# Attention and gate kernel: V and the second query of slot 1 exchange banks and places

## What is computed

```
xn = layernorm(x)
q, k, v = xn @ wq.T, xn @ wk.T, xn @ wv.T          # 32, 8 and 8 heads of 128
q = q * cos + rotate_half(q) * sin ; k likewise
p = softmax(q @ k.T / sqrt(128) * scale + causal)   # four query heads share a k and v
s = (p @ v) @ wo.T
g = silu(sum over the top 2 of 4 experts: gate_e * (xn @ A_e.T @ B_e.T) * 4)
out = x + s * g
```

## Time and profile before

| | us |
|---|---|
| median of 3 runs | 1343.22 |
| lowest and highest run | 1341.77, 1343.50 |
| the profiled execution | 1342.1 |
| its span, first to last instruction | 1340.3 |
| PE, ACT, DVE, POOL busy in it | 1317.3, 971.7, 957.8, 419.9 |
| mean granted clock of PE | 0.994 |

### The profile page before, as it was taken

One profiled execution on the slowest core, in us unless ns is written; L12 is line 12 of the kernel. 1 busy time (PEld: TensorE's weight loads), 2 busy tenths in 40 slices (PEclk: granted clock), 3 DMA queues, 4 the chain that ended last, 5 costly groups with the idle time before them and its releaser, 6 DMA issues.

```text
span 1340.3 us, 22644 instructions
## 1 busy us (share of the span) xinstructions
PE 1317.3 (98%) x7000; PEld 1106.4 (83%) x7000; DVE 957.8 (71%) x2440; ACT 971.7 (72%) x2529; POOL 419.9 (31%) x341
## 2 busy tenths in 40 slices
PE   8899999999999999999999999999999999999996
PEld 7788788878888888888888888888888888888885
DVE  6777587766767677777767677776777767767775
ACT  6977577776768777777777776877777777777673
POOL 5323322333114332223414133141422334133321
PEclk9899999999999999999999999999999999999998
DMA  6000000111001000000101000010100000002223
GB/s 220 9 25 20 25 9 20 53 42 47 31 17 32 16 23 8 16 16 16 31 0 31 0 17 30 0 31 0 31 16 3 29 16 23 8 32 86 84 79 113
DMA packets 23530, 43.66 MB, mean 33 GB/s; under 512 B 2496, under 2 KB 2752, under 8 KB 23488
## 3 DMA queue, kind: packets, MB, share of 16 engines
q1 hardware_dynamic: 20896, 38.74, 9.0%
q10 hardware_dynamic: 2592, 4.40, 0.9%
HBM read 34.74 MB, written 8.39 MB: 32 GB/s over the span
## 4 chain that ended last, share of the span: by engine, by line
PE 94%; ACT 2%; DVE 2%; issue 1%; DMA 0%; ACTq 0%
PE bank_a L487 19%; PE bank_b L487 19%; PE bank_b L581 13%; PE o_ps L581 13%; PE pv_ps L574 10%; PE pair L558 8%; PE pair L565 6%; PE pair L554 2%; PE pair L556 1%; PE o_ps L487 1%; PE bank_a L544 1%; ACT x_sb L945 1%; PE o_ps L534 1%; DVE pT_lo L1204 0%; PE pair L487 0%
## 5 line engine op out<-in xcount | busy, mean ns | idle before, releaser
L391 POOL TENSOR_TENSOR rot<-rot,tab 128x512 f32<-128x512 f32 x160 | 206.7, 1295 | 601.2 <-ACT rot L803 600.9
L871 ACT ACTIVATE pT_hi<-pair 128x768 fp32r<-128x768 f32 x128 | 103.9, 812 | 168.5 <-PE pair L565 167.7
L852 ACT ACTIVATE probs<-probs,row_min 128x128 f32<-128x128 f32 (+1 forms) x512 | 225.6, 447 | 0.1
L863 ACT ACTIVATE probs<-probs,row_inv 128x128 f32<-128x128 f32 (+1 forms) x512 | 190.7, 446 | 22.7 <-DVE row_inv L1234 22.3
L1204 DVE TENSOR_TENSOR pT_lo<-pair,pT_hi 128x768 fp32r<-128x768 f32 x128 | 121.6, 950 | 92.3 <-ACT pT_hi L871 92.0
L374 POOL TENSOR_TENSOR w_hi<-raw,zero 128x512 fp32r<-128x512 f32 x74 | 84.2, 1138 | 247.0 <-PE bank_a L487 131.0
L487 PE MATMUL bank_a<-xT_hi,w_hi 128*128 (+1 forms) x376 | 153.0, 407 | 0.7 <-DVE xT_lo L1073 0.6
L487 PE MATMUL bank_b<-xT_hi,w_hi 128*128 (+1 forms) x376 | 150.3, 400 | 0.0
L1184 DVE TENSOR_TENSOR q_lo<-cosx,q_hi 128x512 fp32r<-128x512 f32 x128 | 117.0, 915 | 44.3 <-ACT q_hi L810 44.1
L487 PE MATMUL bank_a<-xT_hi,w_lo 128*128 (+1 forms) x376 | 146.9, 391 | 0.0
L487 PE MATMUL bank_b<-xT_hi,w_lo 128*128 (+1 forms) x376 | 146.8, 391 | 0.0
(11 more groups left out here) (177 smaller groups left out, 3246.1 us busy)
## 6 DMA issues: line engine op xcount, KB each, us to landing
raw<-w_seq SPq DMA_DIRECT2D x76, 256.0 KB, 2.6
gate_scratch<-b_raw ACTq DMA_DIRECT2D x16, 256.0 KB, 2.0
out<-y_sum SPq DMA_DIRECT2D x16, 256.0 KB, 2.1
x_sb<-x SPq DMA_DIRECT2D x3, 1024.0 KB, 10.8
mid<-x SPq DMA_DIRECT2D x8, 256.0 KB, 2.7
mid<-gate_scratch SPq DMA_DIRECT2D x8, 256.0 KB, 2.9
raw<-x SPq DMA_DIRECT2D x7, 256.0 KB, 2.6
raw<-gate_scratch SPq DMA_DIRECT2D x7, 256.0 KB, 2.8
```

The costliest lines, as they stand in the source:

```text
L391: nc.gpsimd.tensor_tensor(v, v, tab[:, s:s + SEQ].unsqueeze(1).to_broadcast([P, 2, SEQ]), ALU.mult).then_inc(sin_done[kind], 1)
L852: a = nc.scalar.activation(s, s, ACT.Exp, bias=row_min[:, j % 2, i:i + 1], scale=-1.0, accum_out=row_sum[:, i:i + 1])
L863: a = nc.scalar.activation(s, s, ACT.Copy, scale=row_inv[:, i:i + 1])
L871: nc.scalar.activation(pT_hi[:, :, :], pair[j % 2][:, :, 0:ROWS], ACT.Copy).then_inc(pThi_done, 1)
```

## The change

TensorE projects V first, into bank_b, and H2 second, into bank_a. So the projection H3 (bank_b) waits for V's copy instead of H2's cosine product, the projection K (bank_a), and in unit 30 the transposition of V, wait for H2's cosine product instead of V's copy. ScalarE's and VectorE's lists in every unit from 1 on are written in another order; in unit 0 only the copy of V comes ahead of H2's half copies. GpSimd's and SyncE's lists stay.

```diff
@@ -646,18 +646,18 @@
                     bank_free(H0, c2)
                 else:
                     pe.wait_ge(y_added, n4[0])
-                project(H2, bank_b, WQ + 2, x_1, w_1)
+                project(V, bank_b, WV, x_1, w_1)
             pe_side(u, 1, 2)
             if not last:
                 bank_free(H1, c2)
-                project(V, bank_a, WV, x_1, w_1)
+                project(H2, bank_a, WQ + 2, x_1, w_1)
             pe_side(u, 1, 3)
 
 
             pe.wait_ge(probs_ready, n4[3])
             turn_probs(2)
             if not last:
-                bank_free(H2, c2)
+                pe.wait_ge(vT_done, c2)
                 project(H3, bank_b, WQ + 3, x_1, w_1)
             pe_side(u, 2, 0)
             if not last:
@@ -669,7 +669,7 @@
             if ahead:
                 if isinstance(u, int) and u < BLOCKS - 2:
                     pe.wait_ge(xlo_done, BLOCK_TILES * (u + 3))
-                pe.wait_ge(vT_done, c2)
+                bank_free(H2, c2)
                 project(K, bank_a, WK, x_2, w_2)
             pe_side(u, 2, 2)
             if ahead:
@@ -888,51 +888,51 @@
             low_scores(2, n4[3])
             if not last:
                 q_high(H0, c2, n4[3])
-            rows_high(1, n4[2], n4[1])
             attn_high(0, n4[1], None if first else n4[-2])
             exponents(2, n4[3])
+            rows_high(1, n4[2], n4[1])
             act_side(u, 1, 0)
+            low_scores(3, n4[4])
             if not last:
                 swap_halves(H1, bank_a, c2, H0, c2)
-            low_scores(3, n4[4])
             act_side(u, 1, 1)
-            if not last:
-                k_high(c2, n4[4])
             normalise_rows(2, n4[3])
             attn_high(1, n4[2], None if first else n4[-2])
             if not last:
-                swap_halves(H2, bank_b, c2, K, c2)
+                k_high(c2, n4[4])
             act_side(u, 1, 2)
             if not last:
+                copy_vT(c2, c1, bank_b)
                 q_high(H1, c2, n4[3])
             act_side(u, 1, 3)
+            if not last:
+                swap_halves(H2, bank_a, c2, K, c2)
             rows_high(2, n4[3], n4[2])
             exponents(3, n4[4])
             act_side(u, 2, 0)
             if not last:
                 swap_halves(H3, bank_b, c2, H1, c2)
-                copy_vT(c2, c1)
                 low_scores(0, n4[5])
             act_side(u, 2, 1)
-            normalise_rows(3, n4[4])
             if not last:
                 q_high(H2, c2, n4[4])
             attn_high(2, n4[3], None if first else n4[0])
+            normalise_rows(3, n4[4])
             act_side(u, 2, 2)
-            if ahead:
-                swap_halves(K, bank_a, c3, H2, c2)
-            if is_unit(u, 1):
-                b_high()
             if not last:
                 q_high(H3, c2, n4[4])
             if ahead:
                 swap_halves(H0, bank_b, c3, H3, c2)
-            act_side(u, 2, 3)
             rows_high(3, n4[4], n4[3])
+            if ahead:
+                swap_halves(K, bank_a, c3, H2, c2)
             if not last:
                 exponents(0, n4[5])
                 low_scores(1, n4[6])
                 normalise_rows(0, n4[5])
+            act_side(u, 2, 3)
+            if is_unit(u, 1):
+                b_high()
             attn_high(3, n4[4], None if first else n4[0])
             if not last:
                 v_high(c2, n4[4])
@@ -1006,8 +1006,8 @@
             q_high(H1, 2, 3)
             normalise_rows(2, 3)
             act_side(0, 1, 2)
-            swap_halves(H2, bank_b, 2, K, 2)
-            copy_vT(2, 1)
+            copy_vT(2, 1, bank_b)
+            swap_halves(H2, bank_a, 2, K, 2)
             attn_high(1, 2, None)
             act_side(0, 1, 3)
             rows_high(2, 3, 2)
@@ -1265,69 +1265,69 @@
                          start=isinstance(u, int) and u - b < BLOCKS, final=final, bank=(o_ps, bank_b)[t][:, :], xg_set=t)
 
             rows_low(0, n4[1])
+            mask_rows(2, n4[3])
+            attn_low(0, n4[1])
+            if not last:
+                q_low(H0, c2)
             if not first:
                 tile_in(1, 0)
-            mask_rows(2, n4[3])
-            if not last:
-                q_low(H0, c2)
-            if not first:
                 tile_in(1, 1)
             rows_low(1, n4[2])
-            attn_low(0, n4[1])
+            row_inverse(n4[3])
             dve_side(u, 1, 0)
-            row_inverse(n4[3])
+            dve_side(u, 1, 1)
             if not last:
                 cos_product(H1, bank_a, c2, H0, c2)
             mask_rows(3, n4[4])
-            dve_side(u, 1, 1)
             if not last:
                 rotate(H1, c2)
+            dve_side(u, 1, 2)
+            if not last:
                 k_low(c2)
-                cos_product(H2, bank_b, c2)
-            dve_side(u, 1, 2)
-            if not last:
                 q_low(H1, c2)
             dve_side(u, 1, 3)
             rows_low(2, n4[3])
             attn_low(1, n4[2])
-            if not last:
-                rotate(H2, c2)
+            if is_unit(u, 2):
+                split_b()
             if is_unit(u, 1):
                 split_ar()
-            if is_unit(u, 2):
-                split_b()
+            if not last:
+                cos_product(H2, bank_a, c2)
+            dve_side(u, 2, 0)
+            if not last:
+                rotate(H2, c2)
             row_inverse(n4[4])
-            dve_side(u, 2, 0)
             if not last:
                 cos_product(H3, bank_b, c2, H1, c2)
+            dve_side(u, 2, 1)
+            if not last:
+                rotate(H3, c2)
+                q_low(H2, c2)
                 mask_rows(0, n4[5])
-            dve_side(u, 2, 1)
-            if not last:
-                rotate(H3, c2)
             dve_side(u, 2, 2)
             if not last:
-                q_low(H2, c2)
                 q_low(H3, c2)
+            rows_low(3, n4[4])
+            attn_low(2, n4[3])
             if ahead:
                 cos_product(K, bank_a, c3, H2, c2)
-            rows_low(3, n4[4])
-            attn_low(2, n4[3])
-            tile_in(0, 0)
-            if ahead:
                 cos_product(H0, bank_b, c3, H3, c2)
             dve_side(u, 2, 3)
             if not last:
                 row_inverse(n4[5])
+            tile_in(0, 0)
+            if not last:
                 mask_rows(1, n4[6])
             if ahead:
-                rotate(K, c3)
+                rotate(H0, c3)
             attn_low(3, n4[4])
             tile_in(0, 1)
             if ahead:
-                rotate(H0, c3)
-            if not last:
+                rotate(K, c3)
+            if not last:
+                row_inverse(n4[6])
                 v_low(c2)
-                row_inverse(n4[6])
 
         def dve_opening():
 
@@ -1391,7 +1391,7 @@
             k_low(2)
             q_low(H1, 2)
             dve_side(0, 1, 2)
-            cos_product(H2, bank_b, 2)
+            cos_product(H2, bank_a, 2)
             dve_side(0, 1, 3)
             attn_low(1, 2)
             rows_low(2, 3)
```

More of the change, by code:

```diff
@@ L1267, in dve_unit @@
             rows_low(0, n4[1])
-            if not first:
-                tile_in(1, 0)
             mask_rows(2, n4[3])
+            attn_low(0, n4[1])
             if not last:
@@ L1273, in dve_unit @@
             if not first:
+                tile_in(1, 0)
                 tile_in(1, 1)
             rows_low(1, n4[2])
-            attn_low(0, n4[1])
+            row_inverse(n4[3])
             dve_side(u, 1, 0)
-            row_inverse(n4[3])
+            dve_side(u, 1, 1)
             if not last:
@@ L1281, in dve_unit @@
             mask_rows(3, n4[4])
-            dve_side(u, 1, 1)
             if not last:
                 rotate(H1, c2)
-                k_low(c2)
-                cos_product(H2, bank_b, c2)
             dve_side(u, 1, 2)
             if not last:
+                k_low(c2)
                 q_low(H1, c2)
@@ L1292, in dve_unit @@
             attn_low(1, n4[2])
+            if is_unit(u, 2):
+                split_b()
+            if is_unit(u, 1):
+                split_ar()
+            if not last:
+                cos_product(H2, bank_a, c2)
+            dve_side(u, 2, 0)
             if not last:
                 rotate(H2, c2)
-            if is_unit(u, 1):
-                split_ar()
-            if is_unit(u, 2):
-                split_b()
             row_inverse(n4[4])
-            dve_side(u, 2, 0)
             if not last:
                 cos_product(H3, bank_b, c2, H1, c2)
-                mask_rows(0, n4[5])
             dve_side(u, 2, 1)
@@ L1306, in dve_unit @@
                 rotate(H3, c2)
+                q_low(H2, c2)
+                mask_rows(0, n4[5])
             dve_side(u, 2, 2)
             if not last:
-                q_low(H2, c2)
                 q_low(H3, c2)
+            rows_low(3, n4[4])
+            attn_low(2, n4[3])
             if ahead:
                 cos_product(K, bank_a, c3, H2, c2)
```

(4 more changed lines are left out.)

## The result

The changed kernel takes 1353.69 us (median of 4 runs, 1353.07 to 1354.83), the kernel before 1343.34 us beside it: ratio 1.008, 95% interval 1.0067 to 1.0093. It is slower by 10.4 us, where a balance was forecast, and lies outside the range of 1340.5 to 1348.4. The profiled execution took 1353.07 us with a span of 1351.3.

The account below looks back on a forecast made before the run. TensorE, busy 1317.3 of 1340.3 us, was taken as the bound, with 0.24 us a unit to win at K. Gains and losses summed to +0.7 us on 1342.1: 1342.8, or 1343.9 as a median; range 1340.5 to 1348.4.

Parts of the forecast that it names:

- K's gap, -5.3 and -0.3: Projection K follows the last product with V without a gap: 0.24 us in 22 loop units, and 0.3 at 377.52.
- GpSimd keeps its order: Loop: sin(H3) ends later behind weight splits, but VectorE's queue is through before rows_low(3) must start; cost 0, bound 0.3 us.
- Covered waits at H3 and K: Loop: V's copy ends 2.4 us before H3 needs it, H2's cosine product 1.2 us before K does.
- rows_low(2) against scores(0) at 0: Each unit: H2's later half copies still let the low part be ready for scores(0); cost 0, bound 0.1 us a unit.
- the rival of 1347.9: Rival: low part late for scores(0), 0.13 us in 31 units, +4.0 on top of the sum; chance 0.17.
- Unit 3, -1.0: Opening: routing stands before k_low, done 1.8 us sooner, so rows_low(2) ends when scores want it; gain 1.0 us.
- unit 0, +0.7: Opening: H2's two half copies replace one copy, 0.2 us later, ahead of x_high and rows_high(2); loss 0.7 us.
- Starts of units 29 and 30, +1.3 each: tile_in(0,0) behind row_inverse delays mask_rows(1), attn_low(3) and rows_low(0) at ends of units 28 and 29: +1.3, twice.
- tile_in(1,0) and (1,1) ahead of rows_low(1), +0.2 each: Last four units: these steps with their multiplications stand together ahead of rows_low(1) on VectorE; +0.2, twice.
- Unit 30's turn, +0.6: q_high(H2) and attn_high(2) precede normalise_rows(3), so slot 3's transpositions come 0.9 us later; 0.6 left at scores(1).
- unit 31, +2.4: attn_high(2), then four normalisations, precede slot 3's transpositions, so they and all that follows wait: +2.4 us.
- The clock, +0.6: A pause longer by 2.3 us near the end can keep TensorE at half clock longer: +0.6, bounds nothing to 2.8 us.

Follow-up runs that it names:

- run 4: Changed kernel with GpSimd's splits of V's weights held back, in units with i = 3, until rows_low(0) is done: 1346.5 us (1.0032).
- run 1: Kernel before with only ScalarE's copy of V moved ahead of the half copies of H3: 1337.5 us, ratio 0.9958.
- run 8: Changed kernel with GpSimd's residual adds cut to 8 of 512 columns: 1349.0 us (1.0052).
- run 9: Changed kernel with tile_in(0,0) ahead of the cosine products and row_inverse on VectorE in the last four units: 1350.1, 1351.0 and 1352.5 us, ratio 1.006.
- run 11: Kernel before, unedited, traced a second time for its opening: 1343.75 us.
- run 5: Changed kernel with rotate(H0) behind attn_low(3) on VectorE, splits left where they were: 1351.9 us (1.0068).
- runs 3: Changed kernel with GpSimd's split of V's weights moved in the code from the end of i = 2 to the start of i = 3, without a wait: 1353.4 us (1.0079).

## Why the prediction was wrong

- **K's gap, -5.3 and -0.3: right in size, wrong in sum.** Each loop unit that is left alone is 0.23 us shorter. The step that failed is the one that begins "GpSimd keeps its order" and ends "Cost 0, with up to 0.3 us in some 14 units as the bound": GpSimd's splits were followed only as far as sin(H3), where the 0 held. Those of V's weights, at the end of units with i = 2, were not laid beside VectorE's new end of the unit. They stretch mask_rows(1), make attn_low(3) late for output_tile(1,0), and cost 0.8 us in five loop units and in units 3 and 7, 5.6 in all, shown by run 4; the sum had nothing for it.
- **Covered waits at H3 and K, rows_low(2) against scores(0) at 0: right.** No unit waits there, and the new wait in every unit, the rival of 1347.9, did not come. The wait came at another place, one of four units apart.
- **Unit 3, -1.0; unit 0, +0.7.** Unit 3 measured -0.55 without the splits (run 4) and +0.23 with them: scores there still wait 0.30 us for rows_low(2), where the text took the whole 0.67 as gone. Unit 0 measured +0.62, all of it between its third and fourth transpositions (12.6 us for 12.0), where run 1, without the exchange, has 12.0.
- **Starts of units 29 and 30, +1.3 each: right.** Both lose 1.35 us more than before. Of it 0.65 is GpSimd's add (run 8), the rest order.
- **tile_in(1,0) and (1,1) ahead of rows_low(1), +0.2 each: too small.** 0.77 in each of units 29 and 30 and 0.72 in unit 31, 2.26 for the 0.6 of the sum. The sum had the plain 0.7 us for a multiplication; it took 1.29, because the residual add of tile (1,0) starts just before; run 8 gives 0.6 of it back. I had the row for such a stretch and used it for the mask only.
- **Unit 30's turn, +0.6; unit 31, +2.4.** The wait grew by 0.92 in unit 30, and scores(1) took up little of it: in run 9, at full clock, 0.8 was left. Unit 31's grew by 2.26, near the 2.2.
- **The clock, +0.6: too small.** The fall in unit 30 was not foreseen: its outputs and transpositions there cost 1.6 us, and the longer stretch in unit 31 0.5, 2.1 in all. The text named only "from 1320 to 1324, after a pause of 2.6 us" as a place for half clock; the normalisation wait of unit 30, 1.3 us before and 2.2 after, was the second.
- **The side.** The terms missed most are 5.6 us in the loop, 1.65 ahead of scores(3) in the tail and 1.5 of the clock. The first two are places where a long GpSimd instruction meets a VectorE step that a new order has put on the edge. With 0.45 in unit 3 and -0.4 in all else (units 4 to 6 gave 0.56 that was in no term) they lead from +0.7 to +9.5; the two traces differ by 11.0, of which 1.46 is the opening. The chance for slower, 0.29, was held for scores(0), for the clock and the mask at the end, and for K's wait; a stall of the loop by GpSimd's splits was in none of them. The opening is no term of the sum: run 11 has its late start with the kernel before.

The rule of the Trainium skill ("SBUF — State Buffer", section "SBUF: two separate sides") that a VectorE instruction with two SBUF inputs and a GpSimd instruction that reads SBUF shut each other out for the whole instruction is borne out where GpSimd started first: `probs<-probs,tab` took 1.04 us for 0.29, the multiplication 1.29 for 0.69, and `probs<-pair,tab`, whose first input is in PSUM, 0.41 throughout. The chance it left open, that the ratio multiplication in units 28 and 29 starts first, did not occur (1224.06, behind the add at 1223.54, in unit 28).

## What to carry to other kernels

When an order is written anew, lay every engine's list beside it over a whole period, here four units, not one, and give each of the other engine's long instructions its place; a step that is safe in three units of four can stall in the fourth. Look for the smallest edit first: one copy moved ahead of another on ScalarE gave the whole 5.7 us, with no new order to pay for but 0.2 us in each of units 4 to 6. A loop's order is not the order for its last rounds: keep what the last units need apart from it.

## What the runs showed of the hardware

- A 128x4 instruction of VectorE (0.15 us) took 1.26 us when it started 0.05 us behind a GpSimd product of 1.30. A step with a single SBUF input (L1055, 128x4, 0.17 us) took 1.30 beside such a product too (run 11). In the opening one such step goes with a start of unit 0 that is 1.0 to 1.7 us later.
- The granted clock does not follow from one wait alone. The same wait of 2.24 us (2.23 in run 5) ahead of unit 30's transpositions is followed by a fall to half clock in the changed kernel (0.74 and 0.83 of full in the two windows shown) and in runs 3, 4 and 5, and by none in runs 8 and 9, where TensorE had idled 1.1 to 1.2 us less since the start of that unit. What else decides it stays open.
